# Convolution sums in a graph network kernel: four column tiles with 32-column one-hots in place of one 128-column one-hot per edge tile

## The chip, the cores and the metric

One NeuronCore of a Trainium2 chip runs the whole program. The metric is the device time of one execution in microseconds (us); the time of a kernel is the median of its runs. Beside it stands one execution that the hardware profiler recorded, from which all rows below are taken.

## What is computed

A graph of 6250 nodes with 256 features and 100,000 edges, sorted by destination, goes through a first aggregation, a mixture of experts, three graph convolutions and an attention over slices. The change concerns the three convolutions, in short:

```python
for i in range(3):
    h = x @ W[i]
    msg = h[row] * norm[:, None]                 # norm = dinv[row] * dinv[col]; row, col with self loops
    h = segment_sum(msg, col, num_segments=6250) + b[i]
    h = (h - mean(h)) * rsqrt(var(h) + 1e-5) * gamma[i] + beta[i]
    x = relu(h)
```

## The kernel before

**Tiles.** Nodes lie in 49 tiles of 128 (NT), and every node tile has a row block in the accumulator ACC in SBUF, which a layer starts with its self-loop term. Edges lie in 782 tiles of 128 (ET). Of each layer's edges the first TD = 264 tiles, whose destinations fill the first F = 17 node tiles, are handled as dense products: 17 x 49 = 833 products of 128 x 128 pieces of an adjacency matrix (`piece_h`, loaded by SyncE's queue, seven pieces a transfer) with the features X in SBUF.
**A gathered tile.** GpSimd issues an indirect DMA (L2142) that brings the 128 source rows of a tile into slot i mod 24 of the ring `rows_h` (RG = 24). VectorE makes a one-hot of 128 edges x 128 lanes (`hot`, L2238), which has a 1 where an edge's destination, taken modulo 128, is that lane. TensorE multiplies one-hot and rows (L2197) into a PSUM bank; four tiles (G) sum into one bank. After the fourth, `add_group` (L956) adds the bank to ACC in two masked steps, since four tiles may span the border of two node tiles. Every f32 product with 256 columns is two TensorE instructions in the trace, with a weight load each.

**Order and waits.** GpSimd waits, once in four tiles, until the tile 20 to 24 before is consumed (`s_mm`). TensorE starts a layer with 40 dense products (AHEAD_MM); after each gathered tile it runs the dense products that `quota` gives, 1 or 2, until edge tile 738 (DENSE_END), so that the last 44 tiles have none. VectorE follows TensorE tile by tile (the wait on `s_mm` in its main loop), six one-hots ahead (LEAD).

**Node steps.** When all edges of a pair of node tiles are in, the pair ("group", GROUPS from `batches`) is normalised: `sums`, `stats`, `aggregates`, then ScalarE's square root (L2219), `deviations`, `gains`, `shifts` on VectorE; ReLU on ScalarE (L2224); in layers 1 and 2 also two transposes per node tile (`turns`, L2155, 14 edge tiles after the group is due), a copy by ScalarE (L2227), the product with the next layer's weights (`products`, L2165, 18 after), ScalarE's copy into ACC (L2230) and a store to the table in HBM (`store`, 21 after). The second-last group is due at edge tile 764, the last (node tiles 47 and 48) at 784, after all edges. GpSimd starts the next layer's gathers when all stores have landed. The third layer has no transposes, products or stores; VectorE ends it with the residual and its moments.

**Prologue.** Lists and a check that the edges fit this scheme are made by VectorE in `strand`, between its steps for the first node product; where they don't fit, another path would run (`layers_apart`).

## Time and profile before

| | us |
|---|---|
| median of 3 runs | 4605.04 |
| lowest, highest | 4599.81, 4605.38 |
| the profiled execution's own time | 4596.34 |
| its span, first to last instruction | 4594.6 |
| mean granted TensorE clock | 0.91 |

Busy in the profile: TensorE products 85% of the span, weight loads 70%, GpSimd 62%, VectorE 46%, ScalarE 19%. The three convolution layers run from 2199.6 to 4210.7 us, where the last vector step ends. In the rows, PE is TensorE (PEld its weight loads), DVE VectorE, ACT ScalarE, POOL GpSimd and SP SyncE. A timeline row gives start, duration, engine, line, operation, output<-inputs and how many instructions it merges; in brackets the idle time before it and what ended that. A windows row gives the stretch, its length, then the busy time (and count) of PE, PEld, DVE, ACT and POOL, or of the one engine asked for, the granted TensorE clock, the busy share of the DMA engines and GB/s. A groups row ends with busy time, mean ns of one, and idle time before. The profile overlaps consecutive products: one has a duration of 379 ns while they follow each other at shorter distances.

### The profile page before, as it was taken

What the parts mean: (1) busy time and instruction counts of PE and PEld (TensorE: products, weight loads), DVE (VectorE), ACT (ScalarE), POOL (GpSimd) and SP (SyncE); (2) the same over time, 40 slices, a digit from 0 to 9 for tenths busy, and PEclk for the clock granted to TensorE, in tenths of its full rate; (3) what the DMA queues carried; (4) which work ended last, traced back from release to release, by engine and by line L of the source; (5) the groups of instructions that cost most, each with busy time, mean ns of one, the idle gap of its engine ahead of it and who ended that gap; (6) DMA issues with size and microseconds to landing.
All of it is one profiled execution on the core that took longest, in us unless ns stands there. A gap on an engine that the chain in (4) does not pass through costs nothing. (4 is left out here: it accounts for less than half of the span.)

```text
span 4594.6 us, 52816 instructions
## 1 busy us (share of the span) xinstructions
PE 3891.9 (85%) x16777; PEld 3209.9 (70%) x16777; DVE 2100.5 (46%) x6813; ACT 866.6 (19%) x2121; POOL 2871.1 (62%) x2846
## 2 busy tenths in 40 slices
PE   5656666666699999995899998999998999995988
PEld 4544444444488888884788887888886877774657
DVE  5444444454611111116345455454554555555974
ACT  1233333333122222223001011001011000000322
POOL 0377777777168778880677776777776777774000
PEclk8877677777799999997999999999998999997998
DMA  3355555555266666668766666666666666662001
GB/s 106 105 170 168 168 167 164 168 168 167 65 181 188 190 188 188 192 171 272 227 203 200 204 199 208 207 202 202 201 204 204 206 202 204 199 188 69 0 12 57
DMA packets 422939, 779.23 MB, mean 170 GB/s; under 512 B 106971, under 2 KB 264194, under 8 KB 422722
## 3 DMA queue, kind: packets, MB, share of 16 engines
q1 hardware_dynamic: 255078, 433.81, 29.0%
q0 software_dynamic: 160992, 336.12, 26.3%
q10 hardware_dynamic: 6652, 6.67, 0.5%
q8 instruction: 104, 1.70, 0.2%
q14 instruction: 113, 0.93, 0.1%
HBM read 655.55 MB, written 114.39 MB: 168 GB/s over the span
## 5 line engine op out<-in xcount | busy, mean ns | idle before, releaser
L2142 POOL DMA_INDIRECT rows_h<-table,step_src x1554 | 1487.7, 957 | 638.1 <-issue 562.0
L2182 PE MATMUL bank_g<-X,piece_h 128*128 128x256 f32 x4998 | 1314.3, 380 | 14.3 <-DMA piece_h<-edges_A 14.3
L2182 PEld LDWEIGHTS bank_g<-X,piece_h 128*128 128x128 f32 x4998 | 952.0, 190 | 144.8 <-issue 14.7
L2197 PE MATMUL bank_g<-rows_h,hot_h 128*128 128x256 f32 x3108 | 939.7, 390 | 77.6 <-DMA rows_h<-table,step_src 76.9
L887 POOL DMA_INDIRECT rows_r<-table,step_src x782 | 743.1, 950 | 359.3 <-issue 339.2
L912 PE MATMUL bank_r<-rows_r,hots_r 128*128 128x257 f32 x1564 | 578.7, 531 | 382.3 <-ACT rows_r L897 382.0
L2238 DVE TENSOR_SCALAR hot_h<-lane,step_dst 128x128 f32<-128x128 f32 x1554 | 458.6, 302 | 838.4 <-PE bank_g L2197 812.0
L912 PEld LDWEIGHTS bank_r<-rows_r,hots_r 128*128 128x128 f32 x1564 | 394.2, 266 | 546.2 <-ACT rows_r L897 456.0
L2197 PEld LDWEIGHTS bank_g<-rows_h,hot_h 128*128 128x128 f32 x3108 | 591.9, 194 | 193.9 <-DMA rows_h<-table,step_src 116.2
L923 DVE TENSOR_SCALAR hots_r<-lane,step_dst 128x128 f32<-128x128 f32 x782 | 233.9, 306 | 503.2 <-PE bank_r L912 488.9
L1704 POOL DMA_INDIRECT edges_A<-one_d,place_d x264 | 413.4, 1566 | 80.5 <-issue 80.5
L897 ACT ACTIVATE rows_r<-rows_r,step_w 128x256 f32<-128x256 f32 x782 | 339.7, 498 | 639.3 <-DMA rows_r<-table,step_src 639.2
L1663 PE MATMUL pH_e<-xe_e,w_e 128*128 128x256 f32 x1792 | 397.7, 380 | 2.5 <-DMA b_e<-in_L_ffn_b 2.5
L1678 PE MATMUL pY_e<-w_e,h_e 128*128 128x256 f32 x1792 | 396.0, 379 | 0.0
L956 DVE SCALAR_TENSOR_TENSOR ACC<-bank_g,mask,ACC 128x256 f32 x780 | 339.5, 477 | 102.7 <-issue 80.8
L1663 PEld LDWEIGHTS pH_e<-xe_e,w_e 128*128 128x128 f32 x1792 | 341.6, 191 | 49.6 <-issue 2.9
L1678 PEld LDWEIGHTS pY_e<-w_e,h_e 128*128 128x128 f32 x1792 | 336.1, 190 | 43.4
L1638 ACT ACTIVATE h_e<-pH_e,prm_e 128x256 f32<-128x256 f32 x448 | 187.8, 470 | 630.6 <-PE pH_e L1663 630.6
L1606 DVE TENSOR_SCALAR xe_e<-pT_e,prm_e 128x256 f32<-128x256 f32 x114 | 56.7, 539 | 372.6 <-PE pT_e L1670 362.8
L2219 ACT ACTIVATE sd_g<-mv_g,eps 128x2 f32<-128x2 f32 (+1 forms) x75 | 22.1, 295 | 1016.3 <-DVE mv_g L2266 1016.3
L1623 DVE TENSOR_TENSOR y_e<-pY_e,b_e 128x256 f32<-128x256 f32 x112 | 42.3, 419 | 322.4 <-PE pY_e L1678 322.4
L956 DVE SCALAR_TENSOR_TENSOR ACC<-bank_r,mask,ACC 128x257 f32 x392 | 170.7, 477 | 18.0 <-issue 15.3
(318 smaller groups left out, 3039.7 us busy)
## 6 DMA issues: line engine op xcount, KB each, us to landing
piece_h<-edges_A SPq DMA_DIRECT2D x357, 448.0 KB, 3.6
w_e<-in_L_ffn_W SPq DMA_DIRECT2D x112, 1024.0 KB, 8.1
edges_A<-zero_r SPq DMA_DIRECT2D x119, 448.0 KB, 4.9
rows_h<-table,step_src POOLq DMA_INDIRECT x1554, 3.3
got_c<-y SPq DMA_DIRECT2D x14, 896.0 KB, 9.6
rows_r<-table,step_src POOLq DMA_INDIRECT x782, 2.8
table<-ACC SPq DMA_DIRECT2D x48, 256.0 KB
X<-table SPq DMA_DIRECT2D x12, 896.0 KB, 12.1
```

Of the source, the lines that this page charges most:

```text
L887: nc.gpsimd.indirect_dma_start(out=r["rows"][:, x, 0:D], out_offset=None, in_=r["table"][:, :], in_offset=bass.IndirectOffsetOnAxis(ap=c[" ...
L897: act.activation(r["rows"][:, x, 0:D], r["rows"][:, x, 0:D], ACT.Copy, scale=c["step_w"][:, k:k + 1]).then_inc(r["s_scaled"], 1)
L912: pe.matmul(psum[k // G % OH][:, 0:AW], r["hots"][:, k % HOTS, :], r["rows"][:, k % R, 0:AW], start=(k % G == 0), stop=(k % G == G - 1 or ...
L923: v.tensor_scalar(r["hots"][:, k % HOTS, :], c["lane"][:, :], c["step_dst"][:, k:k + 1], None, ALU.is_equal).then_inc(r["s_hot"], 1)
L956: v.scalar_tensor_tensor(out=a, in0=bank[:, 0:width], scalar=c["mask"][:, k, g:g + 1], in1=a, op0=ALU.mult, op1=ALU.add).then_inc(c["ring" ...
L1663: mm = pe.matmul(pH[j][:, n * BR:(n + 1) * BR], w1[:, q, k, o:o + P], xe[:, q, k, :], start=(k == 0), stop=(k == KD - 1))
L1678: mm = pe.matmul(pY[m][:, 0:D], h[:, j, m * P:(m + 1) * P], w2[:, q, j, :], start=(j == 0), stop=(j == HJ - 1))
L1704: nc.gpsimd.indirect_dma_start(out=dram["A"][:, :], out_offset=bass.IndirectOffsetOnAxis(ap=d["place"][:, col:col + 1], axis=0), in_=d["on ...
L2142: nc.gpsimd.indirect_dma_start(out=d["rows"][:, x, :], out_offset=None, in_=tables[l - 1][:, :], in_offset=bass.IndirectOffsetOnAxis(ap=c[ ...
L2182: mm = pe.matmul(pD[o % 2][:, 0:D], d["piece"][:, n % AB, x % PC, :], c["X"][:, ORDER[x // PC] * PC + x % PC, :], start=(x == 0), stop=(x ...
L2197: pe.matmul(pS[i // G % OH][:, 0:D], d["hot"][:, i % HOTS, :], d["rows"][:, x, :], start=(i % G == 0), stop=(i % G == G - 1 or i == GT - 1 ...
L2238: v.tensor_scalar(d["hot"][:, i % HOTS, :], c["lane"][:, :], c["step_dst"][:, TD + i:TD + i + 1], None, ALU.is_equal).then_inc(r["s_hot"], 1)
```

## The change

A block is now eight gathered tiles (GB), four pairs (GP = 2). Each edge's one-hot has 32 columns (`step_low`: destination modulo 32), and a pair sums in one of four column tiles of the TensorE array, that is in 32 of the 128 partitions of a bank (`lanes`). VectorE copies this bank to SBUF (`mid`) and makes one 128 x 128 one-hot (`spread`) from a list `target` that says to which lane each of the 4 x 32 rows belongs (`kept`). One product (`spread` on TensorE) takes the block to its 128 lanes in a second bank, from which `add_group` adds it to ACC (`added`): once in eight tiles where it was once in four. The spreading product of a block comes after the next block's tiles on TensorE, the add after the next copy on VectorE. The check in the prologue asks that two tiles span fewer than 32 nodes. GpSimd's wait comes once in eight tiles. The offset of the high groups' due tile grows from 12 to 16, so the second-last group is due at 768.

```diff
-GG = -(-GT // G)
+GB, GP = 8, 2
+GG = -(-GT // GB)
+LOW = P // 4
+EP = -(-ET // GP)
...
-    out = [(t, 2, 16 * (t + 2) + SLACK) for t in range(F, NT - 2, 2)]
+    out = [(t, 2, 16 * (t + 2) + 2 * GB) for t in range(F, NT - 2, 2)]
...
-            pe.matmul(pH[:, 0:EG], firsts[:, :], dcol[:, 0:EG * G:G], start=True, stop=True).then_inc(s_head, 1)
+            pe.matmul(pH[:, 0:EP], firsts[:, :], dcol[:, 0:EP * GP:GP], start=True, stop=True).then_inc(s_head, 1)
...
                 if t == 0:
                     then(v.tensor_copy(lane_i[:, 0, :], dcol[:, 0:ET]))
-                    then(v.tensor_scalar(lane_i[:, 1, :], lane_i[:, 0, :], P - 1, None, ALU.bitwise_and))
+                    v.tensor_scalar(lane_i[:, 1, :], lane_i[:, 0, :], P - 1, None, ALU.bitwise_and)
+                    then(v.tensor_scalar(low_i[:, TD:ET], lane_i[:, 0, TD:ET], LOW - 1, None, ALU.bitwise_and))
                 elif t == 1:
+                    done(v.tensor_copy(c["step_low"][:, :], low_i[:, TD:ET]))
+                    v.memset(base[:, :, :], 0.0)
...
+                    v.tensor_copy(pairs, pH[:, 0:EP])
+                    for k in range(4):
+                        heads = pH[k * LOW:(k + 1) * LOW, TD // GP + k:EP:4]
+                        v.tensor_copy(base[k * LOW:(k + 1) * LOW, 0, 0:heads.shape[1]], heads)
...
+                elif t == 7:
+                    then(v.tensor_scalar(base_i[:, 0, :], base[:, 0, :], -1.0, part[:, 0:1], ALU.mult, ALU.add))
+                    then(v.tensor_scalar(base_i[:, 1, :], base_i[:, 0, :], LOW - 1, None, ALU.bitwise_and))
+                    then(v.tensor_copy(base[:, 1, :], base_i[:, 1, :]))
+                    then(v.tensor_tensor(base_i[:, 0, :], base[:, 0, :], base[:, 1, :], ALU.add))
+                    then(v.tensor_scalar(base_i[:, 1, :], base_i[:, 0, :], P - 1, None, ALU.bitwise_and))
+                    v.tensor_copy(c["target"][:, :], base_i[:, 1, :])
...
-                    if i % Q == 0 and i >= RG:
-                        g.wait_ge(r["s_mm"], n - RG + Q)
+                    if i % GB == 0 and i >= RG:
+                        g.wait_ge(r["s_mm"], n - RG + GB)
...
+            def lanes(l, h):
+                n, tiles = ET + (l - 1) * GT, tiles_of(h)
+                m = (l - 1) * GG + h
+                for x in sorted({i % RG // Q for i in tiles}):
+                    last = max(i for i in tiles if i % RG // Q == x)
+                    pe.wait_ge(r["s_row"][x], 16 * (BEFORE[x] + (l - 1) * EACH[x] + landed(last, GT, RG, x)))
+                pe.wait_ge(r["s_hot"], n + tiles[-1] + 1)
+                if m >= 2:
+                    pe.wait_ge(d["s_mid"], m - 1)
+                for i in (*tiles[0::GP], *tiles[1::GP]):
+                    k = i % GB // GP * LOW
+                    pe.matmul(pA[m % 2][k:k + LOW, 0:D], d["hot"][:, i % (2 * GB), :], d["rows"][:, i % RG, :],
+                              start=(i % GP == 0), stop=(i % GP == GP - 1), tile_position=(0, k)).then_inc(r["s_mm"], 1)
+            def spread(l, h):
+                m, k = (l - 1) * GG + h, rows_of(h)
+                pe.wait_ge(d["s_mid"], m + 1)
+                if m >= 2:
+                    pe.wait_ge(r["s_add"], 2 * (EG + m - 1))
+                pe.matmul(pR[m % 2][:, 0:D], d["spread"][0:k, m % 2, :], d["mid"][0:k, m % 2, :],
+                          start=True, stop=True).then_inc(d["s_spread"], 1)
...
-                    pe.matmul(pS[i // G % OH][:, 0:D], d["hot"][:, i % HOTS, :], d["rows"][:, x, :],
-                              start=(i % G == 0), stop=(i % G == G - 1 or i == GT - 1)).then_inc(r["s_mm"], 1)
+                    s = TD + i
+                    if i % GB == 0:
+                        lanes(l, i // GB)
+                        if i >= GB:
+                            spread(l, i // GB - 1)
                     dense(l, AHEAD_MM if i == 0 else quota(s - 1), quota(s))
...
+                spread(l, GG - 1)
...
             def hot(i):
-                v.tensor_scalar(d["hot"][:, i % HOTS, :], c["lane"][:, :], c["step_dst"][:, TD + i:TD + i + 1], None,
+                v.tensor_scalar(d["hot"][:, i % (2 * GB), :], c["lane"][:, 0:LOW], c["step_low"][:, i:i + 1], None,
                                 ALU.is_equal).then_inc(r["s_hot"], 1)
+            def kept(l, h):
+                m, k = (l - 1) * GG + h, rows_of(h)
+                v.wait_ge(r["s_mm"], ET + (l - 1) * GT + tiles_of(h)[-1] + 1)
+                v.tensor_scalar(d["spread"][:, m % 2, :], c["lane"][:, :], c["target"][:, h:h + 1], None, ALU.is_equal)
+                v.tensor_copy(d["mid"][0:k, m % 2, :], pA[m % 2][0:k, 0:D]).then_inc(d["s_mid"], 1)
...
+                v.wait_ge(d["s_spread"], m + 1)
+                v.wait_ge(r["s_add"], 2 * (EG + m))
+                add_group(c, v, pR[m % 2], g, offs[h], D)
...
-                    if i >= 2:
-                        v.wait_ge(r["s_mm"], first + i - 1)
-                    if i + LEAD < GT:
-                        hot(i + LEAD)
+                    if i % GB == 0 and h >= 1:
+                        kept(l, h - 1)
+                        if h >= 2:
+                            added(l, h - 2)
+                    if i + GB < GT:
+                        hot(i + GB)
...
+                for h in range((GT + 1) // GB, GG):
+                    kept(l, h)
+                for h in range((GT + 1) // GB - 1, GG):
+                    added(l, h)
```

How the rows of the engines' programs move is shown at three places, first before, then with the change. A row is line, operation and shape as written in the source (an f32 product counts once, xN merges N alike).

TensorE in the middle of layer 1, before and after: dense products (`piece_h`), gathered tiles (`rows_h`), transposes (`ident`).

```order
L2197 MATMUL bank_g<-rows_h,hot_h 128x256
L2182 MATMUL bank_g<-X,piece_h 128x256 x2
L2197 MATMUL bank_g<-rows_h,hot_h 128x256
L2182 MATMUL bank_g<-X,piece_h 128x256 x2
L2155 MATMUL bank_g<-ident,xin_h 128x128 x4
L2197 MATMUL bank_g<-rows_h,hot_h 128x256
L2182 MATMUL bank_g<-X,piece_h 128x256
```

```order
L2239 MATMUL bank_g<-mid_h,spread_h 128x256
L2213 MATMUL bank_g<-X,piece_h 128x256 x12
L2186 MATMUL bank_g<-ident,xin_h 128x128 x4
L2213 MATMUL bank_g<-X,piece_h 128x256 x2
L2230 MATMUL bank_g<-rows_h,hot_h 32x256 x8
L2239 MATMUL bank_g<-mid_h,spread_h 128x256
L2213 MATMUL bank_g<-X,piece_h 128x256 x5
L2196 MATMUL bank_g<-w_g,xt_h 128x256 x4
L2213 MATMUL bank_g<-X,piece_h 128x256 x8
```

The gathered tiles now stand in blocks of eight with 32-row outputs, each followed by the spreading product of the block before (L2239), and the dense products of eight tiles run together.

TensorE at the end of layer 1, up to the next layer's first dense products; L2155 and L2186 are the transposes, L2165 and L2196 the node products.

```order
L2155 MATMUL bank_g<-ident,xin_h 128x128 x2
L2197 MATMUL bank_g<-rows_h,hot_h 128x256 x4
L2165 MATMUL bank_g<-w_g,xt_h 128x256 x2
L2197 MATMUL bank_g<-rows_h,hot_h 128x256 x16
L2155 MATMUL bank_g<-ident,xin_h 128x128 x4
L2197 MATMUL bank_g<-rows_h,hot_h 128x256 x3
L2165 MATMUL bank_g<-w_g,xt_h 128x256 x4
L2155 MATMUL bank_g<-ident,xin_h 128x128 x4
L2165 MATMUL bank_g<-w_g,xt_h 128x256 x4
L2182 MATMUL bank_g<-X,piece_h 128x256 x40
```

```order
L2239 MATMUL bank_g<-mid_h,spread_h 128x256
L2186 MATMUL bank_g<-ident,xin_h 128x128 x2
L2196 MATMUL bank_g<-w_g,xt_h 128x256 x2
L2230 MATMUL bank_g<-rows_h,hot_h 32x256 x8
L2239 MATMUL bank_g<-mid_h,spread_h 128x256
L2230 MATMUL bank_g<-rows_h,hot_h 32x256 x6
L2239 MATMUL bank_g<-mid_h,spread_h 128x256 x2
L2186 MATMUL bank_g<-ident,xin_h 128x128 x4
L2196 MATMUL bank_g<-w_g,xt_h 128x256 x4
L2186 MATMUL bank_g<-ident,xin_h 128x128 x4
L2196 MATMUL bank_g<-w_g,xt_h 128x256 x4
L2213 MATMUL bank_g<-X,piece_h 128x256 x40
```

The second-last group's transposes stood three tiles before the last gathered tile and now stand behind the last spreading product.

VectorE in the middle of layer 1, around one add (at the ISA rows the source sets registers for the next step).

```order
L2238 TENSOR_SCALAR hot_h<-lane,step_dst 128x128
L2244 TENSOR_TENSOR ACC<-bank_g,ACC 128x256
L2238 TENSOR_SCALAR hot_h<-lane,step_dst 128x128 x2
L956 ISA
L956 SCALAR_TENSOR_TENSOR ACC<-bank_g,mask,ACC 128x256
L956 ISA
L956 SCALAR_TENSOR_TENSOR ACC<-bank_g,mask,ACC 128x256
L2271 RECIPROCAL rs_g<-sd_g 128x2
L2238 TENSOR_SCALAR hot_h<-lane,step_dst 128x128
L2276 SCALAR_TENSOR_TENSOR z_h<-z_h,mv_g,vec_g 128x256 x2
L2238 TENSOR_SCALAR hot_h<-lane,step_dst 128x128
```

```order
L2355 SCALAR_TENSOR_TENSOR z_h<-z_h,rs_g,vec_g 128x256 x2
L2297 TENSOR_SCALAR spread_h<-lane,target 128x128
L2298 COPY mid_h<-bank_g 128x256
L979 ISA
L979 SCALAR_TENSOR_TENSOR ACC<-bank_g,mask,ACC 128x256
L979 ISA
L979 SCALAR_TENSOR_TENSOR ACC<-bank_g,mask,ACC 128x256
L2290 TENSOR_SCALAR hot_h<-lane,step_low 128x32 x5
L2324 SCALAR_TENSOR_TENSOR z_h<-ACC,dinv,vec_g 128x256 x2
L2290 TENSOR_SCALAR hot_h<-lane,step_low 128x32
L2331 BN_STATS stat_g<-z_h 128x6 x2
L2290 TENSOR_SCALAR hot_h<-lane,step_low 128x32
```

Before, each one-hot waits for a tile of TensorE and the add comes once in four tiles; now the one-hot `spread_h` and the copy `mid_h` open a block, the add of the block before follows, and the eight one-hots come without a wait of their own.

## Rows read from the trace of the kernel before

**Rows 1.** the page: part 1 (busy us, share, instructions) and one group of part 5
```profile
PE 3891.9 (85%) x16777; PEld 3209.9 (70%) x16777; DVE 2100.5 (46%) x6813; ACT 866.6 (19%) x2121; POOL 2871.1 (62%) x2846
...
L887 POOL DMA_INDIRECT rows_r<-table,step_src x782 | 743.1, 950 | 359.3 <-issue 339.2
```

**Rows 2.** windows, L2142 alone, by layer, then layer 1 in two parts
```profile
2199.56:2852.03 652.47, 494.93 (x517) 0.99 0.69 211
2872.57:3524.18 651.61, 494.08 (x518) 0.99 0.68 206
3544.09:4197.51 653.42, 495.89 (x517) 0.98 0.63 192
...
2200.80:2223.30 22.50, 17.01 (x18) 0.84 0.98 339
2223.30:2852.90 629.60, 477.80 (x499) 0.99 0.68 207
```

**Rows 3.** waits of GpSimd over the three layers: us, times, longest us
```profile
POOL rows_h L2142 <- issue: 562.0, 1429, 126.9
...
POOL rows_h L2142 <- PE bank_g L2197: 37.5, 123, 0.3
```

**Rows 4.** windows and groups of 2300 to 2500 us: busy, mean ns
```profile
2300.00:2500.00 200.00, 200.00 (x942) 176.07 (x942) 100.97 (x326) 18.01 (x49) 151.55 (x160) 1.00 0.67 201
...
L2182 PE MATMUL bank_g<-X,piece_h 128*128 128x256 f32 x536 | 142.0, 379 | 0.0
L2197 PE MATMUL bank_g<-rows_h,hot_h 128*128 128x256 f32 x322 | 95.8, 379 | 0.0
L2165 PE MATMUL bank_g<-w_g,xt_h 128*128 128x256 f32 x56 | 13.2, 379 | 0.0
...
L2182 PEld LDWEIGHTS bank_g<-X,piece_h 128*128 128x128 f32 x537 | 102.0, 190 | 13.9
...
L2238 DVE TENSOR_SCALAR hot_h<-lane,step_dst 128x128 f32<-128x128 f32 x160 | 47.3, 302 | 82.2 <-PE bank_g L2197 81.7
L956 DVE SCALAR_TENSOR_TENSOR ACC<-bank_g,mask,ACC 128x256 f32 x81 | 35.3, 477 | 8.4 <-issue 8.4
```

**Rows 5.** timeline of TensorE, first tile of layer 1: start us, us
```profile
2223.41 0.59 PE L2197 MATMUL bank_g<-rows_h,hot_h 128*128 128x256 f32 x2
```

**Rows 6.** timeline of all engines, boundary of layers 1 and 2
```profile
2852.03 0.95 POOL L2142 DMA_INDIRECT rows_h<-table,step_src  x1 [0.30 <-issue]
...
2855.07 1.06 PE L2155 MATMUL bank_g<-ident,xin_h 128*128 128x128 f32 x4
...
2857.41 1.89 PE L2165 MATMUL bank_g<-w_g,xt_h 128*128 128x256 f32 x8
...
2859.34 0.84 ACT L2230 ACTIVATE ACC<-bank_g,dinv 128x256 f32<-128x256 f32 x2 [2.52 <-PE bank_g L2165]
...
2861.54 0.30 ACT L2219 ACTIVATE sd_g<-mv_g,eps 128x2 f32<-128x2 f32 x1 [1.36 <-DVE mv_g L2266]
...
2865.49 3.78 PE L2165 MATMUL bank_g<-w_g,xt_h 128*128 128x256 f32 x8 [0.47 <-ACT xt_h L2227]
...
2872.57 0.94 POOL L2142 DMA_INDIRECT rows_h<-table,step_src  x1 [19.59 <-DMA table<-ACC]
```

**Rows 7.** timeline of all engines, end of layer 3
```profile
4187.56 3.63 PE L2197 MATMUL bank_g<-rows_h,hot_h 128*128 128x256 f32 x8 [3.10 <-DMA rows_h<-table,step_src]
...
4197.51 0.94 POOL L2142 DMA_INDIRECT rows_h<-table,step_src  x1 [0.30 <-issue]
...
4201.61 1.13 PE L2197 MATMUL bank_g<-rows_h,hot_h 128*128 128x256 f32 x4 [0.16 <-DMA rows_h<-table,step_src]
...
4204.64 0.88 DVE L2253 SCALAR_TENSOR_TENSOR z_h<-ACC,dinv,vec_g 128x256 f32<-128x256 f32 x2
```

**Rows 8.** windows, last 40 us of gathers in layer 3
```profile
4160.00:4200.00 40.00, 24.35 (x65) 16.85 (x65) 20.49 (x68) 0.29 (x1) 29.32 (x31) 0.76 0.37 110
```

**Rows 9.** timeline of VectorE, prologue
```profile
65.25 0.97 DVE L409 TENSOR_TENSOR falls<-now_i,next_i 128x782 f32<-128x782 int32 x1 [2.22 <-DMA deg_i<-in_dst]
```

More of the change, by code:

```diff
@@ L82 @@
 SLACK = 12
-LANES, DOUBTS = 6, 15
+LANES, DOUBTS = 7, 16
 def quota(s):
@@ L417, in strand @@
                 elif t == 6:
-                    v.tensor_reduce(bad[:, 2:3], wide[:, :], AX.X, ALU.add)
+                    v.tensor_reduce(bad[:, 2:3], wide, AX.X, ALU.add)
                     v.tensor_reduce(bad[:, 3:4], need[:, :], AX.X, ALU.add)
@@ L1806, in convolutions @@
                          xt=sb("xt_h", [P, 2, D], F32, own))
-                d.update(rows=sb("rows_h", [P, RG, D], F32, own), hot=sb("hot_h", [P, HOTS, P], F32, own),
+                d.update(rows=sb("rows_h", [P, RG, D], F32, own), hot=sb("hot_h", [P, 2 * GB, LOW], F32, own), mid=sb("mid_h", [P, 2, D], F32, own),
+                         spread=sb("spread_h", [P, 2, P], F32, own),
                          piece=sb("piece_h", [P, AB, PC, P], F32, own), bank=bank)
```

60 lines of the change are left out of this document (31 added, 29 removed).

## The prediction

> **What bounds the kernel now.** I read the page first: TensorE is busy 85% of the span and GpSimd 62% [rows 1], which makes TensorE look like the bound. The change touches the three convolution layers alone (and a few steps of the prologue), so I cut the trace by layer. The windows over the gathers show what to see: from the first to the last gather the layers take 652.47, 651.61 and 653.42 us [rows 2], 518 gathers each, so 1.26 us per gather, in all three alike, although the third layer has no node products on TensorE. Next the waits of GpSimd: nearly all its idle time is "issue", and where the ring's wait on TensorE is named, the longest is 0.3 us [rows 3], which is the gap that stands between any two gathers. So GpSimd never stood still for TensorE: **the gathers' own cadence, 0.95 us and 0.30 us of issue, is the bound**, for 1958 of 4595 us. TensorE runs beside it at almost the same pace: in 200 us it is busy all 200, with 942 instructions at 0.212 us [rows 4]. It is a second bound just under the first, with a ring of 24 tiles between them. Outside the gathers are two boundaries between layers (20.54 us from the last gather of layer 1 to the first of layer 2, [rows 6]) and the end of layer 3, 13.2 us from its last gather (4197.51, [rows 7]) to the end of its last vector step at 4210.7; these are chains of single steps.
>
> **The change, part by part.** Terms are against the profiled run, 4596.34 us; the runs' median, 4605.04, stands 8.7 us above, and the sum is carried over to it. About 9 us (0.2%) either way is what a measurement can tell from no change.
>
> *Gathers.* Same number, same sizes, same queue. The ring's wait comes once in eight tiles instead of once in four and asks for the block issued three blocks before. Cost 0 while TensorE keeps up.
>
> *TensorE per block of 8 tiles.* In the 200 us of [rows 4] 161 tiles passed. For 8 tiles: dense products 536/161 x 8 = 26.6 instructions x 0.2155 = 5.74 us; node products 56/161 x 8 x 0.2155 = 0.60; transposes, the 28 that are left of the 942, 28/161 x 8 at half that, 0.15; gather products 16 x 0.2155 = 3.45. Sum 9.94 against 10.08 of GpSimd. Afterwards the 16 stay 16 (two passes each) but go to four column tiles, and one full product (2 x 0.2155 = 0.43) is added. What 16 instructions on column tiles cost, the trace does not show. Lower end: four at once, 4 x 0.2155 = 0.86. Upper end: one after another, 3.45, plus two drains where the array changes its form, each at most a product's duration less its spacing (379 - 213 = 166 ns, [rows 4]), 0.33 together. I take the value between: the two passes of one tile must follow each other, while the second overlaps the first pass of the next tile: 9 steps x 0.2155 = 1.94, plus 0.33. Block: 5.74 + 0.75 + 0.43 + 2.27 = 9.19 us. TensorE gains 0.75 us a block, some 49 us a layer, and **all of it turns into waiting for rows**, since the gathers set the pace. The Trainium skill, TensorEngine Tiling (Array Packing), section Theoretical Speedup, gives up to 4x for outputs of 32 columns; by that the 16 take 0.86 us and the block 8.1, and the gathers would still set the end. Its section Tiling Modes says that a change of form drains the array; no row here shows such a change.
>
> *The ring.* Block h+3 may start once the products of block h are done. Layer 1 is tightest: TensorE starts tile 0 at 2223.41 [rows 5], GpSimd wants to start tile 24 at 2199.56 + 24 x 1.26 = 2229.8. With 2 us for the block, 4 us are left, and they grow by 0.9 a block. VectorE is no longer paced tile by tile: it runs to the next place where it needs TensorE or ScalarE (a dense sum, a square root), which can lie up to eight tiles ahead of TensorE's order. Behind such a wait stand its one-hots for the next block. It is some microseconds late then, TensorE with it, and these slacks hide it. Its work shrinks anyway: two adds of 0.48 us less per block and eight narrower one-hots (0.30 us each now, [rows 4]), against 0.30 + 0.48 for the new one-hot and the copy, which reads a bank as an add does. Cost 0; without the slack each would cost 1 to 3 us.
>
> *Boundaries: the new exposed part.* Before, the last rows land 4.10 us after their gather was issued (4197.51 to 4201.61, [rows 7]) and only the last product and add stand behind them. Now the last six tiles start together, then copy, spreading product, add. From the last gather, at half clock (eight instructions took 3.63 us at this very place, [rows 7]; in the last 40 us the clock was 0.76, [rows 8], and TensorE will have less to do): landing 4.1; 12 instructions in 7 steps x 0.427 = 3.0, tail 0.17; one-hot and copy 0.7 (0.30 + 0.48 less what follows on overlaps); spreading product 0.85 + 0.17: 9.0. In layer 3 two adds of which the last shows (0.88) bring 9.9 us, where it was 7.1 (4204.64, [rows 7]): +2.8; at full clock 8.0, +0.9.
> In layers 1 and 2 something else is late: the transposes and products of the second-last node group move behind this spreading product, since that group is due 4 steps later, and ScalarE serves that group before it takes the last group's square root. From 9.0: transposes 1.06, copy 0.4, products 3.78 at half clock, ScalarE's two copies 0.84 (durations of [rows 6]): 15.1, where the square root stood at 9.5 (2861.54, [rows 6]). That is +5.6 a boundary. At full clock (products 1.89, steps half as long) it is 11.2, +1.7. The clock was mixed here before (both 1.89 and 3.78 occur, [rows 6]); with less TensorE work I lean to half: +4.3. Sum: 2 x 4.3 + 2.8 = **+11.4 us**, ends 4.3 and 14.
>
> *Prologue.* VectorE gets about ten short steps. Those of its steps 0 to 2 (some 1900 columns, 2.3 us by the 0.97 us of a 782-wide step, [rows 9]) fall before a wait of 2.22 us for a transfer [rows 9]; those of step 7 before a stretch where it waits for TensorE. +0.5, ends 0 and 5.
>
> *Gathers under VectorE.* Before VectorE starts in layer 1, 18 gathers take 17.01 us (0.945 each); after that 499 take 477.80 (0.9575) [rows 2]. So VectorE costs 12.5 ns x 1536 = 19 us over the layers. What part of that is the one-hots' is open; in the first aggregation, which has them but not the node steps, a gather has 950 ns [rows 1], so at most 5 ns, 8 us. They get narrower but not fewer: -2.5, ends 0 and -19.
>
> Sum +11.4 + 0.5 - 2.5 = +9.4: 4605.7 in the profiled run's terms, **4614 against the median**.
>
> **Rivals.**
> *A, slower by more: the column tiles do not overlap* (the change does not do what it says). For: no row shows any overlap of two products. Then a block is 5.74 + 0.75 + 0.43 + 3.45 + 0.33 = 10.70 us against 10.08. Over the 59 blocks up to where the dense products end that is 37 us, less 5 of slack, in layers 1 and 2 (the third, without node products, is level at 9.95): +64, 4679; without drains 4638. It decides from 2.8 us per block for these 16. Chance 0.12.
> *B, the loads come out from behind the products.* In the window of [rows 4] 942 loads of 0.19 us, all to the same rows, lie wholly beside the 200 us of products. With column tiles each load might stand before its product: 16 x 0.19 = 3.0 us more, a block of 13.7, so 3.6 x 59 a layer: +600 us, 5200. The Trainium skill, TensorE: Matmul & The Clock Gate, Part 3, says that a load overlaps running products only where the row group differs, and column tiles share it; the loads of this trace contradict that. Chance 0.02.
> *C, a mid-layer clock drop.* TensorE now pauses about 1 us a block; where its clock falls to 1.2 GHz a block costs up to 18 us and eats the ring's slack. It would then be busy again and recover. For: at 24 of 40 us busy it had 0.76 [rows 8]. Against: the pauses are short and the dense work stays. +15 to +40, 4640. Chance 0.04.
> *D, not slower: the gathers speed up.* If the narrow one-hots and fewer adds take most of the 19 us away and the boundaries stay at full clock (+4), the sum is -14: 4591. It decides once gathers average 949 ns or less. Against: gathers are longer here than in the first aggregation (957.5 against 950, [rows 1, 2]), and what VectorE does here and not there are the node steps, which stay. Chance 0.08.
>
> **How the numbers follow.** Forecast 0.74, A 0.12, B 0.02, C 0.04, D 0.08. The forecast's own range is +4.3 - 4 to +14 + 5, so 4605 to 4624, and half of it lies past the 0.2% line (4614.3): slower 0.74/2 + 0.18 = 0.55, same 0.37 + 0.01 = 0.38, faster 0.07. The range for all: down to 4599 for part of D, up to 4650 for C and the mild half of A.
>
> **What would show it.** Right: each layer again 650 to 655 us from first to last gather, no GpSimd wait on TensorE over 0.3 us, TensorE idle some 50 us more per layer, waiting for rows; the boundaries 24 to 26 us; the third layer's end 3 us longer. Wrong: GpSimd waiting for the column-tile products (A, B, C, told apart by their spacing and the clock), a gather mean under 950 ns (D), or boundaries as short as before.

## The result, and the profile after

| | us |
|---|---|
| median of 11 runs, changed kernel | 4614.16 (4609.72 to 4619.06) |
| median of 11 runs, kernel before, same chip | 4603.04 (4598.86 to 4609.18) |
| ratio | 1.0023, 95% interval 1.0014 to 1.0032 |
| profiled execution, changed | 4619.06, span 4617.1, clock 0.887 |

The forecast was 4614.0, with a slowdown of over 0.2% as the likeliest sign. Against the kernel before it meant +9 us, where the medians of eleven runs differ by 11.1 us; that the two times themselves agree to 0.2 us is luck, since the median of the kernel before went from 4605.04 (3 runs) to 4603.04 (11 runs). Note that the profiled execution of the changed kernel is the slowest of its eleven, 5 us above the median, while that of before (4596.34) is below all of these eleven; a plain difference of the two spans (22.5 us) is twice what the runs show.

The page of the changed kernel: the span and the groups that answer to [rows 1] (line engine op, count, busy us, mean ns, idle before and its cause).

```profile
span 4617.1 us, 53636 instructions
...
PE 3611.8 (78%) x17167; PEld 2824.7 (61%) x17167; DVE 1891.8 (41%) x6827; ACT 865.7 (19%) x2121; POOL 2880.2 (62%) x2847
...
L2173 POOL DMA_INDIRECT rows_h<-table,step_src x1554 | 1493.2, 961 | 645.6 <-issue 601.7
...
L910 POOL DMA_INDIRECT rows_r<-table,step_src x782 | 745.6, 954 | 355.4 <-issue 332.9
...
L2230 PE MATMUL bank_g<-rows_h,hot_h 128*32 128x256 f32 x3108 | 243.7, 434 | 363.2 <-issue 314.4
```

TensorE fell from 85% to 78% of the span, VectorE from 46% to 41%, and the time did not fall. The windows from first to last gather of each layer (stretch, length, busy us and count of PE, PEld, DVE, ACT, POOL, clock, DMA share, GB/s) answer to [rows 2]:

```profile
2207.66:2861.74 654.08, 547.53 (x3086) 427.25 (x3086) 253.48 (x1048) 58.23 (x161) 496.46 (x517) 0.93 0.69 210
2883.16:3536.09 652.93, 546.38 (x3071) 425.19 (x3069) 251.72 (x1032) 58.22 (x161) 495.32 (x517) 0.94 0.68 206
3560.21:4216.40 656.19, 510.62 (x2805) 387.66 (x2803) 286.24 (x1169) 7.10 (x24) 498.58 (x518) 0.90 0.63 192
```

The layers take 654, 653 and 656 us where they took 652, 652 and 653. TensorE is idle more than 100 us in each. The waits of the three layers say for what (us in total, times, longest):

```profile
POOL rows_h L2173 <- issue: 601.7, 1551, 129.1
...
DVE ACC L2314 <- PE bank_g L2213: 385.9, 47, 26.4
PE bank_g L2230 <- issue: 314.4, 140, 7.6
...
PE bank_g L2230 <- DMA rows_h<-table,step_src: 37.4, 10, 9.8
...
PE bank_g L2230 <- DVE hot_h L2290: 10.5, 7, 3.5
```

TensorE's idle time stands before the column-tile products (L2230): it waits until a block's eighth row tile is in. GpSimd waits for TensorE once, 0.3 us, where [rows 3] had 123 such gaps. The rows call most of TensorE's idle time "issue", which names no releaser. The start times do: the first product of a block follows the start of the block's eighth gather by 4.0 to 4.1 us in the median of each layer (65 blocks each, counted from the trace). So the gathers' cadence is the bound, in the open now.

What 16 column-tile instructions take, at full and at half clock (timeline of TensorE, start and duration; the spreading product follows at once):

```profile
2300.87 1.07 PE L2230 MATMUL bank_g<-rows_h,hot_h 128*32 128x256 f32 x16 [1.16 <-issue]
...
2301.87 0.70 PE L2239 MATMUL bank_g<-mid_h,spread_h 128*128 128x256 f32 x2
```
```profile
4201.45 1.94 PE L2230 MATMUL bank_g<-rows_h,hot_h 128*32 128x256 f32 x16 [6.52 <-issue]
...
4203.31 1.22 PE L2239 MATMUL bank_g<-mid_h,spread_h 128*128 128x256 f32 x2
```

The next product starts 1.00 us after the first of 16, and 1.86 at half clock: four lie beside each other. One after another they would take 3.45 us, so this is 3.4 times faster. The rule that the prediction set against its own value (the Trainium skill, TensorEngine Tiling (Array Packing), Theoretical Speedup, up to 4x for 32 columns) agrees with this trace; 2.27 us was too high. Both changes of the array's form show, and are small: the 1.00 us is 0.14 more than 4 x 0.2155, and in the 34 blocks that TensorE reached without idle time the first column-tile product starts 0.31 us after the product before it, 0.09 more than one spacing. Together that is 0.23 us, where the prediction allowed at most 0.33.

The second boundary, from the last gather of layer 2 to the first of layer 3, against [rows 6]:

```profile
3536.09 0.95 POOL L2173 DMA_INDIRECT rows_h<-table,step_src  x1 [0.30 <-issue]
3539.50 1.93 PE L2230 MATMUL bank_g<-rows_h,hot_h 128*32 128x256 f32 x12 [5.05 <-issue]
3541.36 2.08 PE L2239 MATMUL bank_g<-mid_h,spread_h 128*128 128x256 f32 x4
...
3543.22 1.06 PE L2186 MATMUL bank_g<-ident,xin_h 128*128 128x128 f32 x4
3543.80 0.88 DVE L979 SCALAR_TENSOR_TENSOR ACC<-bank_g,mask,ACC 128x256 f32 x2 [0.21 <-DVE ACC L979]
3544.32 0.66 ACT L2279 ACTIVATE xt_h<-bank_g 128x256 f32<-128x256 f32 x2 [10.54 <-PE bank_g L2186]
3544.76 3.69 PE L2196 MATMUL bank_g<-w_g,xt_h 128*128 128x256 f32 x8 [0.47 <-ACT xt_h L2279]
...
3546.48 0.25 DVE L2337 BATCH_NORM_AGGREGATE mv_g<-stat_g 128x2 f32<-128x6 f32 x2
3548.48 0.84 ACT L2282 ACTIVATE ACC<-bank_g,dinv 128x256 f32<-128x256 f32 x2 [3.50 <-PE bank_g L2196]
3549.21 0.29 ACT L2271 ACTIVATE sd_g<-mv_g,eps 128x2 f32<-128x2 f32 x1
...
3560.21 0.95 POOL L2173 DMA_INDIRECT rows_h<-table,step_src  x1 [23.17 <-DMA table<-ACC]
```

This is the chain that was forecast: the moments of the last group are ready at 3546.7, but its square root (L2271) stands behind ScalarE's two copies for the second-last group, whose products ran at half clock (3.69 us). It starts 13.1 us after the last gather, where in the first boundary of before it was 9.5. In the first boundary of the changed kernel those products take 1.99 us, the square root starts at 11.1 us, and little is lost behind the vector chain.

### The profile page after: what moved, and what is told of

Its sections match the earlier page's. It is cut to its first block and busy times, and to the rows that moved or that the text cites. A ratio compares the mean times of both kernels' runs of the same rounds, so it can differ in the third digit from the quotient of the medians.

```text
span 4617.1 us, 53636 instructions
## 1 busy us (share of the span) xinstructions
PE 3611.8 (78%) x17167; PEld 2824.7 (61%) x17167; DVE 1891.8 (41%) x6827; ACT 865.7 (19%) x2121; POOL 2880.2 (62%) x2847
## 5 line engine op out<-in xcount | busy, mean ns | idle before, releaser
L2213 PE MATMUL bank_g<-X,piece_h 128*128 128x256 f32 x4998 | 1171.3, 391 | 14.3 <-DMA piece_h<-edges_A 14.3
L2213 PEld LDWEIGHTS bank_g<-X,piece_h 128*128 128x128 f32 x4998 | 987.8, 198 | 162.2 <-issue 15.9
L935 PE MATMUL bank_r<-rows_r,hots_r 128*128 128x257 f32 x1564 | 565.7, 521 | 397.0 <-ACT rows_r L920 396.6
L2230 PE MATMUL bank_g<-rows_h,hot_h 128*32 128x256 f32 x3108 | 243.7, 434 | 363.2 <-issue 314.4
L2230 PEld LDWEIGHTS bank_g<-rows_h,hot_h 128*32 128x32 f32 x3108 | 101.4, 118 | 471.9 <-issue 451.0
L2290 DVE TENSOR_SCALAR hot_h<-lane,step_low 128x32 f32<-128x32 f32 x1554 | 292.4, 255 | 21.0 <-issue 21.0
L2297 DVE TENSOR_SCALAR spread_h<-lane,target 128x128 f32<-128x128 f32 x195 | 58.9, 302 | 477.4 <-PE bank_g L2230 477.3
L979 DVE SCALAR_TENSOR_TENSOR ACC<-bank_g,mask,ACC 128x256 f32 x390 | 170.5, 478 | 77.8 <-issue 56.3
L2271 ACT ACTIVATE sd_g<-mv_g,eps 128x2 f32<-128x2 f32 (+1 forms) x75 | 22.1, 295 | 906.6 <-DVE mv_g L2337 906.5
L2314 DVE TENSOR_TENSOR ACC<-bank_g,ACC 128x256 f32<-128x256 f32 x51 | 21.7, 425 | 385.9 <-PE bank_g L2213 385.9
```

Source lines behind the costliest of these rows:

```text
L935: pe.matmul(psum[k // G % OH][:, 0:AW], r["hots"][:, k % HOTS, :], r["rows"][:, k % R, 0:AW], start=(k % G == 0), stop=(k % G == G - 1 or ...
L2213: mm = pe.matmul(pD[o % 2][:, 0:D], d["piece"][:, n % AB, x % PC, :], c["X"][:, ORDER[x // PC] * PC + x % PC, :], start=(x == 0), stop=(x ...
L2230: pe.matmul(pA[m % 2][k:k + LOW, 0:D], d["hot"][:, i % (2 * GB), :], d["rows"][:, i % RG, :], start=(i % GP == 0), stop=(i % GP == GP - 1) ...
L2290: v.tensor_scalar(d["hot"][:, i % (2 * GB), :], c["lane"][:, 0:LOW], c["step_low"][:, i:i + 1], None, ALU.is_equal).then_inc(r["s_hot"], 1)
```

## The experiments

The twelve runs fell on three chips. On the first, where the first four ran, the kernel before takes 4594.22 us (median of 29 runs), much as in the result. On the other two it takes 5051 us, and the eight runs there are read apart below.

**The change once more, as the measure.** No edit.

> The changed kernel as it is, as the measure for the runs beside it. Theory T (the gathers' cadence is the bound, what TensorE saves turns into waiting for rows; the loss of some 11 us comes from the two boundaries and the end of layer 3, +7 us, and from longer gathers, +5 to +6): ratio to the kernel before 1.001 to 1.0035, layers of 652 to 657 us from first to last gather, boundaries 21 to 25 us, and the stretch before the layers (8.1 us longer in the one profiled run after) within 3 us of the kernel before, since the code there is the same. Rival R1 (the loss lies ahead of the layers): the first gather of layer 1 again 8 us later than before, boundaries and layers as before. Rival R2 (switching and column tiles cost TensorE the time): GpSimd waits for TensorE over 0.3 us somewhere.

4603.81 us, ratio 1.0020 (1.0011 to 1.0029). Layers 653.73, 653.68, 655.87; boundaries 21.70 and 21.17; first gather at 2206.59. GpSimd's waits name TensorE nowhere.

**Only the prologue.**

```diff
--- the kernel before
+                    v.tensor_copy(pairs, pH[:, 0:EP])
+                    for k in range(4):
+                        heads = pH[k * LOW:(k + 1) * LOW, TD // GP + k:EP:4]
+                        v.tensor_copy(base[k * LOW:(k + 1) * LOW, 0, 0:heads.shape[1]], heads)
...
+                elif t == 7:
```

> The kernel before with only what the change adds ahead of the layers (the pair heads, four shifted copies, the second table of lanes, step 7, one more affine_select); the layers are those of before. Theory T: +0 to +1 us, ratio within 0.1% of 1. Rival R1: +8 us (1.0018), with the first gather of layer 1 some 8 us later.

4595.36 us, ratio 1.0000 (0.9991 to 1.0009). R1 falls. The first gather was at 2203.85 here; over the six traces with 4600 us it lies anywhere between 2199.6 and 2207.7, the 2200.14 of the next experiment among them, which has all of the changed kernel's code ahead of the layers. The 8 us that the pair of traces shows there is spread between executions and no cost of the change.

**The column-tile products twice.**

```diff
-                for i in (*tiles[0::GP], *tiles[1::GP]):
+                for again in range(2):
+                    for i in (*tiles[0::GP], *tiles[1::GP]):
...
+                        if again == 1:
+                            mm.then_inc(r["s_mm"], 1)
```

> Each pass over the column tiles is issued a second time, only the last lets the copy go; the result is the same. That gives TensorE about 1.0 us more per block of eight tiles, 195 us in all. Theory T: TensorE waits for rows about 2 us per block, so that this is hidden: same time as the changed kernel within 0.2%, only the three ends of layers longer by 1 us each (+3 us), and the waits for rows shorter by some 190 us. Rival R2 (TensorE's time on the column tiles is exposed, the chance that I called A): +100 to +200 us. If the extra busy time keeps TensorE's clock up at the boundaries, those get shorter by 1 to 3 us.

4608.07 us (4605.62 to 4610.68), 4.3 us above the changed kernel on the same chip. Its groups over the three layers, column-tile and spreading products:

```profile
L2231 PE MATMUL bank_g<-rows_h,hot_h 128*32 128x256 f32 x6216 | 423.2, 415 | 255.3 <-issue 213.7 <-DMA rows_h<-table,step_src 22.8 <-DVE hot_h L2293 18.4
...
L2242 PE MATMUL bank_g<-mid_h,spread_h 128*128 128x256 f32 (+1 forms) x390 | 144.3, 455 | 0.0
```

3108 more instructions make this group 174 us longer and shorten TensorE's waits for rows from 346 us (311.6 and 34.3 in the repeat of the changed kernel) to 237; the layers stay at 651.29, 652.15 and 656.15 us. TensorE as a whole is only 99 us busier in the gather stretches (1709 against 1610), because its clock rose with the work, 0.93, 0.93 and 0.90 to 0.97, 0.98 and 0.94 by layer, and its other products got shorter (the spreading products 455 ns against 524). That is why the waits shrink by 109 us and not by some 190. The boundaries grow to 23.23 and 23.58 us, from 21.2 to 21.7 in the three of the changed kernel whose node products took 1.99 us, as they do here. The last block's products took 3.57 us there, 1.71 more, at half clock; that the clock would help there is not borne out. So R2 falls: between the ends of layers, even twice these products cost nothing, and what the change saves on TensorE there is worth nothing on this chip.

**Vector steps with one input.**

```diff
-                    v.scalar_tensor_tensor(out=z[:, u, :], in0=c["ACC"][:, t + u, 0:D], scalar=dinv(t + u),
-                                           in1=row(0, l), op0=ALU.mult, op1=ALU.add).then_inc(q["z"], 1)
+                    v.tensor_scalar(z[:, u, :], c["ACC"][:, t + u, 0:D], dinv(t + u), None, ALU.mult).then_inc(q["z"], 1)
...
```

> The changed kernel, where the scaling, the centring and the last scaling of the layer norm read one tensor (tensor_scalar) instead of two: it leaves out the bias, gamma and beta of the three convolutions. Same count and width of VectorE steps, same chain. Theory T2 (gathers get longer where VectorE steps that read two SBUF tensors run, which is where the excess over 0.945 us comes from): gathers fall from 0.961 to about 0.948 us on average, no gather of 1.5 us is left, the three layers take some 6 us less each: -15 to -20 us. Rival (any VectorE step costs the gathers the same, or the long ones come from TensorE or DMA): mean 0.957 or more, time within 5 us of the changed kernel.

4594.49 us, 9.3 us less than the changed kernel on the same chip. It leaves out the bias, gamma and beta of the three convolutions. Windows of the gathers alone (length, GpSimd busy):

```profile
2207.27:2854.59 647.32, 489.84 (x517) 0.94 0.69 212
2875.50:3523.44 647.94, 490.48 (x517) 0.93 0.68 207
3544.48:4194.13 649.65, 492.14 (x518) 0.91 0.63 194
```

All three layers are 6 us shorter, by GpSimd's busy time (496.1, 496.1 and 498.3 before), not by its gaps: a gather takes 0.948 to 0.952 us instead of 0.960 to 0.964. So steps that read two tensors in SBUF do lengthen gathers that run beside them, in place and sign as theory T2 has it. The edit also shortens the steps themselves, from 477 to 480 ns down to 362 to 388, which the expectation did not say. The length alone is not the cause: the adds (L979) take 478 ns too, read one tensor in PSUM and one in SBUF, and leave gathers as they are (counted below). The size is 18 us in the traces and 9 us in the medians, since the changed kernel's profiled execution was again its slowest (4613.79, 10 us above its median); 3 of the 18 us are a difference in gathers that nothing disturbs. The place where it is seen best is the changed kernel of the result (timeline of VectorE and GpSimd):

```profile
3015.20 0.87 DVE L2324 SCALAR_TENSOR_TENSOR z_h<-ACC,dinv,vec_g 128x256 f32<-128x256 f32 x2
3015.22 1.69 POOL L2173 DMA_INDIRECT rows_h<-table,step_src  x1 [0.30 <-issue]
```

A gather that starts 20 ns after such a pair begins lasts until 0.8 us after the pair's end. The Trainium skill, SBUF — State Buffer, Who interferes with whom, has VectorE and GpSimd share one pair of ports, and a VectorE instruction with two SBUF inputs contend with a GpSimd one that reads SBUF. If issuing an indirect gather counts as such a read, since its offsets (`step_src`) lie in SBUF, it has to wait by that rule, and the 1.69 us here agrees. The same section lists `tensor_scalar` among the steps that can take the shared ports as well, so by it the one-input form need not be free, and it is not: gathers beside it take 959 ns, and 945.5 beside no vector step.

Which steps disturb a gather can be counted from the traces. A gather with a two-input step anywhere beside it goes to the third column, of the others one with a one-hot beside it to the last; the excess is over the mean of the gathers with no vector step beside them in the same trace.

| trace | beside none, ns | beside two-input steps: count, excess in us | beside one-hots, excess in us |
|---|---|---|---|
| before | 945.5 | 292, 14.8 | 3.7 |
| only the prologue | 948.0 | 297, 14.0 | 3.2 |
| changed, the result | 948.3 | 296, 18.7 | 1.0 |
| changed, once more | 947.4 | 284, 20.0 | 1.0 |
| products twice | 945.4 | 283, 19.7 | 1.1 |
| one input | 945.5 | 32, 2.3 (one-input steps: 242, 3.4) | 0.4 |

Gathers with nothing beside them but adds and copies, which read a PSUM bank and at most one tensor in SBUF, lie within 0.5 ns of the first column. The change makes the one-hots' part smaller by 2.4 us and the two-input steps' part larger by 5, at the same number of disturbed gathers: each is disturbed for longer. Gathers over 1.3 us are two in before and none in the prologue-only kernel, seven, nine and nine in the three traces with the change, two with one input. The 32 gathers still disturbed there lie beside the residual add of layer 3, which keeps its two inputs. I take the bunched order of VectorE (it now runs ahead to the next place where it needs another engine) for the cause; no kernel here kept the two inputs and spread the steps out, so that part is argued, not shown. The first column also moves by up to 3 ns between traces, the same kernel's layers included (before and prologue-only). That is over 4 us for 1554 gathers, and no cost of any edit.

**The other chips.** There, the changed kernel was run again, and the one-input steps in the kernel before:

> The changed kernel once more, as the measure for the three beside it; the four runs before this call fell on a chip where the kernel before took 5051 us and whose gathers waited for TensorE and for their rows. Where the kernel before takes about 4600 us: ratio 1.001 to 1.0035. Where it takes about 5050 us again: rows land late there, the ring of 24 tiles is then what sets the pace, and the change, which wants all eight tiles of a block landed and gives eight slots back at a time, should lose 0.5 to 1%.

> The same one-tensor steps in the kernel before (bias, gamma and beta of the three convolutions left out). The changed kernel's gathers came to 1944.9 us over the three layers with them, from 1963.3. If the change's longer gathers come only from the bunching of the two-tensor steps, the kernel before falls to the same 1942 to 1947 us from 1957.5, and the two differ only by boundaries and end, +3 to +6 us. If something else in the change lengthens gathers (copies, wide one-hots of the spreading product, the wait once in eight), the kernel before falls further, to 1938 to 1941.

The changed kernel takes 5089.41 us against 5050.74: 1.0078 (1.0063 to 1.0092), four times the loss on the first chip. The size is inside what was expected for this case; the reason given there, that rows land late, is not shown (below). The one-input kernel before takes 5047.01 us (0.9990, 0.9981 to 0.9999); its layers are 757.50, 747.92 and 744.74 us, so the question it was made for cannot be read here. One of the pauses that these chips show, in its timeline:

```profile
2700.72 0.95 POOL L2142 DMA_INDIRECT rows_h<-table,step_src  x1 [0.30 <-issue]
...
2701.97 0.95 POOL L2142 DMA_INDIRECT rows_h<-table,step_src  x1 [0.30 <-issue]
...
2702.30 1.07 PE L2182 MATMUL bank_g<-X,piece_h 128*128 128x256 f32 x3 [0.32 <-issue]
2705.15 0.48 DVE L2238 TENSOR_SCALAR hot_h<-lane,step_dst 128x128 f32<-128x128 f32 x2 [2.57 <-remote]
2705.18 0.80 SPq L2083 DMA_DIRECT2D piece_h<-edges_A  x2
2705.27 0.66 ACT L2227 ACTIVATE xt_h<-bank_g 128x256 f32<-128x256 f32 x2 [14.06 <-remote]
2705.55 0.94 POOL L2142 DMA_INDIRECT rows_h<-table,step_src  x1 [2.64 <-remote]
```

Between 2703.0, the start of the last of the three products, and 2705.1 no engine starts anything, then all start within 0.6 us. Gaps of over 1.7 us from gather to gather are 44 to 49 a layer in either of these two kernels, one in 16 us, where the traces of the first chip show 0 to 7. Most are not like the one above: the four engines together start nothing for over 2 us in 10 of the 143 gaps of the one-input kernel before, and in 77 of them TensorE never pauses for over 1.2 us. Against one gather each 1.26 us the gaps cost 106, 96 and 93 us a layer in the one-input kernel before and 123, 119 and 102 us in the changed one: no more gaps, but more long ones, six of 6 to 10 us against a single one (12.3 us, near the start of layer 1). For the changed kernel, GpSimd's waits and one such gap:

```profile
POOL rows_h L2173 <- remote: 201.7, 98, 4.7
POOL rows_h L2173 <- PE bank_g L2230: 186.0, 49, 9.2
```
```profile
2676.93 0.94 POOL L2173 DMA_INDIRECT rows_h<-table,step_src  x1 [0.30 <-issue]
2682.13 0.95 POOL L2173 DMA_INDIRECT rows_h<-table,step_src  x1 [4.26 <-PE bank_g L2230]
```

On these chips the ring of 24 is often full: GpSimd waits for TensorE 49 times, 186 us in all. The changed kernel asks for eight landed tiles before it multiplies the first, gives slots back in eights, and finds TensorE at a lower clock (0.83 to 0.86 over its layers, 0.93 to 0.95 in the other). Which of these three makes the gaps longer was not tried apart. The trace speaks against the first: a block's first product starts 19 to 20 us in the median after its eighth gather (4.0 to 4.1 on the first chip), and TensorE waits for rows once, for 4.4 us, so the rows have long landed. What pauses these chips stays open.

**TensorE's free time spent: F = 19.** Two more node tiles by dense products, 32 gathered tiles fewer a layer.

```diff
-F = 17
+F = 19
```

> The kernel before with F = 19, the same exchange of 32 gathered tiles for 98 dense products per layer. Before, TensorE had 9.94 us of work in 10.08 us of gathers. 98 more products of 0.43 us are 42 us more, 32 tiles fewer 14 us less: TensorE's 640 us becomes some 670 us, above 612 us of gathers. Theory T: layers of 655 to 675 us, GpSimd waits for TensorE by several us at a time, and with the 60 us of the scatters +60 to +120 us: slower, where the changed kernel gets faster by the same exchange. If the layers here too come out at 612 us, the change was not needed for that and TensorE's saving is worth nothing at F = 19 either.

> The changed kernel with F = 19: two more buckets of nodes go to dense products instead of gathers, so 32 gathered tiles fewer per layer and 98 dense products more. Theory T (the freed TensorE time is only waiting for rows): a layer is 486 gathers of 1.26 us = 612 us instead of 654, some 40 us less, if TensorE keeps up; it needs 98 x 0.43 = 42 us more per layer, of the some 100 us (314 us of waits for gathers in three layers, 386 with all its waits) it has. The two dense buckets cost GpSimd 32 more scatters of 1.9 us ahead of the layers (+60 us) in a stretch where it is the bound. Together -120 + 60 = -60 us, -40 to -90: about 4545. Rival R2 (TensorE is still the second bound right under the first): layers shrink by under 15 us each, and the sum is +15 to +60.

> The kernel before with F = 19 (two more buckets of nodes by dense products). The earlier run shows +58 us ahead of the layers for the 32 more scatters. On a chip with 4600 us, theory T: TensorE was busy 635 of 652 us per layer, and gets 98 x 0.43 - 64 x 0.2155 = +28 us: 660 us and more against 612 us of gathers, so the layers stay at 655 to 670 us and the sum is +60 to +110 us (1.013 to 1.024). If instead the layers shrink to some 612 to 620 us, TensorE was no second bound and F = 19 gains without the change as well.

> The changed kernel with F = 19. TensorE was busy 548 of 653 us per layer at a clock of 0.93; plus 98 x 0.43 less 4 blocks x 1.5 = +36 us, so 584 us against 612 us of gathers. Theory T: layers of 612 to 620 us, -105 to -125 us, +58 us ahead of the layers: -45 to -65 us against the changed kernel with F = 17, that is 0.988 to 0.993 of the kernel before. Rival R2: GpSimd waits for TensorE, layers of 635 us or more, and nothing is gained.

All four are on the 5051 us chips, each edit on both. Before with F = 19: 4978.92 and 4971.28 us, 0.9859 (0.9845 to 0.9873) and 0.9846 (0.9834 to 0.9859). Changed with F = 19: 5029.00 and 5026.53 us, 0.9950 and 0.9951 (0.9938 to 0.9964). I expected the opposite: F = 19 to pay only with the change. The windows of the kernel before with F = 19 show why not:

```profile
2395.80:3111.15 715.35, 671.27 (x3065) 579.59 (x3066) 290.02 (x974) 57.06 (x157) 465.33 (x486) 0.97 0.63 194
3136.73:3846.05 709.32, 669.82 (x3057) 576.90 (x3056) 285.90 (x966) 57.73 (x158) 466.90 (x485) 0.97 0.62 191
3870.25:4571.00 700.75, 635.70 (x2795) 532.81 (x2793) 314.68 (x1099) 6.80 (x23) 468.09 (x485) 0.97 0.59 183
```

On these chips a gather costs 1.45 us with its share of the pauses, not 1.26, so 32 fewer should save 46 us a layer. Against the one-input kernel before, the nearest trace with F = 17, the layers are 42, 39 and 44 us shorter; TensorE's 671 us find room in 715, and the scatters ahead of the layers cost 57 us once: 125 less 57 is 68 us, where the runs gave 72 and 79. With the change the gain is 63 us (5089 to 5027), without it 79 on the same chip (5051 to 4971), so TensorE's saving bought nothing here either. On a 4600 us chip, where a layer has 612 us for those 671, this was not run and stays open. **The fastest version on these chips is the kernel before with F = 19.**

**The order at the ends of layers.**

```diff
+                    if i // GB == GG - 1 and i % GB == 0 and l < LAYERS:
+                        turns(l, len(GROUPS) - 2)
+                        products(l, len(GROUPS) - 2)
```
```diff
--- the changed kernel with F = 19
+                        if last:
+                            spread(l, i // GB - 1)
                         lanes(l, i // GB)
...
+                added(l, GG - 2)
+                kept(l, GG - 1)
+                added(l, GG - 1)
```

> The changed kernel, where TensorE does the transposes and products of the second-last node group ahead of the last block's column-tile products and not behind the last spreading product, in layers 1 and 2. Theory T (this order is what makes the boundaries longer): each boundary 2 to 3 us shorter, so -3 to -6 us in all. Rival: ScalarE or VectorE reach that group too late anyway, the products then hold up the last block, and the boundaries stay or grow by 1 to 2 us.

> F = 19 and the change, and the second-last block's spreading product and adds of a layer are done ahead of the last block's column-tile products, copy and product. In the boundary of the changed kernel these two adds (0.88 us) and their wait stood in the chain between the last gather and the node steps. Theory T: 1.0 to 1.5 us less at each of three ends of layers, -3 to -4 us against F = 19 alone. Rival (ScalarE's own work for the second-last group, which ends at the same time, holds the square root): 0 to -1 us.

The first takes 5091.65 us (1.0080), against 1.0078 for the changed kernel on the other of these chips; its boundaries are 27.6 and 28.0 us against 24.4 and 24.6. The rival holds, by 3 us a boundary where it said 1 to 2. Its first boundary, after a last gather at 3112.05:

```profile
3121.37 1.99 PE L2196 MATMUL bank_g<-w_g,xt_h 128*128 128x256 f32 x8 [0.47 <-ACT xt_h L2279]
3123.29 1.06 PE L2230 MATMUL bank_g<-rows_h,hot_h 128*32 128x256 f32 x12
```

The last block waits for the node products, and starts 11.2 us after the gather; in the changed kernel on such a chip it was 7.8 us (3121.62 less 3113.84). The second takes 5032.30 us against 5026.53 for F = 19 alone: no gain, and its two boundaries (33.8 and 23.8 us) are too scattered by the pauses to tell 1 us.

## Why the prediction was right

All is against the trace of before, so spread between executions counts. The sum is best taken from the first gather to the span's end, and over two traces of either kind (before and prologue-only; the result's and its repeat):

| stretch | old layers | changed | difference | forecast |
|---|---|---|---|---|
| the three gather stretches | 1957.5, 1960.2 | 1963.2, 1963.3 | +4.4 | -2.5 |
| the two boundaries | 40.45, 37.97 | 45.54, 42.87 | +5.0 | +8.6 |
| last gather to the span's end | 397.1, 399.9 | 400.7, 399.2 | +1.5 | +2.8 |
| sum | | | +10.9 | +8.9 |

The prologue's +0.5 measured 0.0. The medians gave +11.1 and +9.6 us. The boundaries lie wholly apart (18.6 to 20.5 us in the old layers, 21.2 to 24.1 changed); the gathers do only in layer 3, and the last row is within what one kernel's traces differ by. The kernel with the products twice, left out of the table, has 1959.6 us in the gather stretches: as many disturbed gathers as the changed kernel, at the lower level of the undisturbed ones (945.4 ns).

- *The bound* and *the ring*: right. Gathers set the pace, and GpSimd waits for TensorE no more than once, 0.3 us; even twice the column-tile work left that so. This holds for the first chip and that of the result, not for the two others, where GpSimd does wait for TensorE.
- *TensorE per block*: direction right, size off. Busy 635 us of layer 1 became 548, that is 9.8 to 8.5 us for 8 tiles, a gain of 1.3 us where 0.75 was forecast. The step that was mis-sized is the nine spacings for 16 column-tile instructions: they take four, and with a drain 1.00 us at full clock, not 2.27. Part of that gain was taken back by the clock, which fell from 0.99 to 0.93 in the layers. As forecast, all of it became waiting for rows.
- *Boundaries*: path right. Taken by the node products' clock, the sum was close too: at full clock (1.99 us, three boundaries of four in the two traces) the boundary grew by 1.8 us where +1.7 was forecast, at half clock (3.69 us, the fourth) by 4.5 where +5.6 was. The forecast leaned to half, +4.3, and that choice accounts for most of the 3.6 us by which the two boundaries stayed below it. Inside the sum, errors cancel. Landing took 3.3 to 3.5 us, not 4.1. The reading of [rows 7] was right, the last update for those rows comes at 4201.57, but it was one of the later ones: landings in that trace have a median of 3.3 us and reach 6.7. The 12 column-tile instructions took 1.86 us, not 3.0, and they ran at half clock in all four boundaries, the ones with fast node products too.
- *End of layer 3*: the adds of the last block started 7.7 us after the gather (4224.06 less 4216.40), and the node steps at 8.64 us, where 9.9 stood in the forecast and 7.13 before.
- *Gathers under VectorE*: the term that came out wrong. Narrower one-hots do relieve the gathers, by 2.4 us, just what was forecast (-2.5). What the prediction put at nothing is the new order of the node steps with two inputs, which it saw only as steps "which stay": their excess went from 14.4 to 19.4 us, +5. Another +1.7 of the measured +4.4 is the level of undisturbed gathers in the four traces, which no edit set. In the layers' lengths the cost is sure in layer 3 alone: 656.2, 655.9 and 656.2 us in three traces with the change, 653.4 and 653.6 in two without; layers 1 and 2 overlap (651.3 to 654.1 against 651.6 to 653.7).
- So the mechanism held, but that the total was met to 2 us is luck in part: the ends cost 5 us less than forecast, the gathers 7 more.
- *Rivals*: A and B fell by the 1.00 us for 16 instructions; D fell, since only the one-hots' 3 us of the 19 were there to be won, and taking the second input away gives what it promised in another way (9 us). C was half right: the clock did fall, and the gathers never noticed.

## What to carry to other kernels

Before making a busy engine faster, look for the engine that never waits for it: here GpSimd, whose idle gaps are all "issue", set the pace, and some 90 us a layer saved on TensorE bought nothing. Coarser blocks are paid at every end of a layer; the same change cost 0.2% in the result and on the first chip and 0.8% on another, so test a change of this kind on more than one. When the engine that issues gathers is the bound, look at what runs on VectorE beside it, and how many SBUF tensors that reads. And before two traces are compared for a few microseconds, compare something in them that the change cannot touch, as the undisturbed gathers here.

## What the runs showed of the hardware

- f32 products on four column tiles of 32 run four at a time: 16 instructions in 1.00 us at full clock, 1.86 at half, then a full-width product at once. Going to column tiles costs 0.09 us and coming back 0.14.
- An indirect gather whose issue takes 0.95 us takes up to 1.69 when it starts just behind a pair of vector steps with two SBUF inputs. Steps of the same 478 ns that read PSUM and one SBUF tensor leave it at 0.95; one-input steps add 14 ns.
- Chips differ: one program takes 4594 us on the first chip (4603 in the result) and 5051 on two others, where gathers pause once in 16 us.
- A profiled execution can be the slowest of a kernel's runs: it was for four of the five kernels on the 4600 us chips that ran after before, by 3 to 10 us over the median.
